# Another order of the first two tiles' work in the opening attention of a two-layer network

## The reference, cut to what matters

```
features_n = rmsnorm(features, fn_w)                 # rows of ctx
Q = rmsnorm(layernorm(x) @ Wq.T + Wq_b, qn_w)
K = rmsnorm(features_n @ Wk.T + Wk_b, kn_w)
attn = softmax(Q @ K.T / sqrt(512))                  # 64 x 64 in each of 32 sequences
x = x + attn @ features_n
...                                                  # sparse ffn, second attention, gated ffn
```

## Time and profile before

| | |
|---|---|
| median of 3 runs | 1487.09 us (1485.61 to 1487.6) |
| span of the profiled execution | 1487.2 us; no other time of that execution is given |
| PE busy | 1456.9 us, 98% of the span |
| DVE, ACT, POOL busy | 1121.6, 793.4 and 708.2 us |
| mean granted clock of TensorE | 0.999 |
| first 45 us: busy PE, DVE, ACT, POOL | 36.9, 27.1, 27.0, 28.7 us |

### The profile page before, as it was taken

The page is one execution under the profiler, slowest core; times in us unless marked ns, Lnnn a source line. Parts: engine busy times, 40 slices in busy tenths (PEclk is TensorE's granted clock), DMA queues, the critical chain, the costliest instruction groups (busy, mean ns, idle before and its releaser), DMA issues.

```text
span 1487.2 us, 27765 instructions
## 1 busy us (share of the span) xinstructions
PE 1456.9 (98%) x9948; PEld 851.1 (57%) x9948; DVE 1121.6 (75%) x2161; ACT 793.4 (53%) x3201; POOL 708.2 (48%) x668
## 2 busy tenths in 40 slices
PE   8999999999999989999999999999999999999998
PEld 6888645555555555556555555655555565555554
DVE  5887787888877878676776776777677677677868
ACT  5678731211123776565556646655754664565663
POOL 6678885554665453344233434333343433343553
PEclk9999999999999999999999999999999999999999
DMA  5744445443444585534443543543454345234523
GB/s 191 239 150 141 128 90 116 106 94 82 75 82 72 118 167 90 125 86 76 110 79 66 108 99 54 102 89 78 89 93 89 82 84 106 51 66 70 103 48 114
DMA packets 359225, 148.98 MB, mean 100 GB/s; under 512 B 342336, under 2 KB 342720, under 8 KB 356144
## 3 DMA queue, kind: packets, MB, share of 16 engines
q1 hardware_dynamic: 357792, 139.87, 44.2%
q10 hardware_dynamic: 1296, 7.34, 1.5%
HBM read 60.11 MB, written 4.19 MB: 43 GB/s over the span
## 4 chain that ended last, share of the span: by engine, by line
PE 49%; DVE 6%; ACT 5%; POOL 3%; DMA 2%; SPq 1%; issue 1%; DVEq 0%; POOLq 0%; ACTq 0%
PE bank L72 16%; PE bank L73 15%; PE bank L74 15%; ACT a_prob L1977 3%; PE bank L2649 2%; DMA a_kT_lo<-a_kn_lo 2%; ACT a_oT_lo L1954 1%; POOL a_qrs L1849 1%; DVE a_oT_lo L2246 1%; ACT a_qr_hi L1951 1%; POOL a_prob L1831 1%; DVE a_kn L2201 1%; DVE a_qve L2185 1%; DVE x_res L2169 1%; DVE x_res L2333 1%
## 5 line engine op out<-in xcount | busy, mean ns | idle before, releaser
L1977 ACT ACTIVATE a_prob<-a_prob,a_nmx 128x64 f32<-128x64 f32 x512 | 170.2, 334 | 250.0 <-DVE a_nmx L2222 249.9
L1831 POOL TENSOR_TENSOR a_prob<-a_prob,a_mask 128x512 f32<-128x512 f32 x64 | 79.9, 1269 | 278.4 <-DVE a_prob L2216 278.4
L72 PE MATMUL bank<-w,xT_hi 128*128 128x448 f16 (+1 forms) x512 | 187.5, 366 | 1.1 <-PEq L1043 1.1
L74 PE MATMUL bank<-w,xT_hi 128*128 128x448 f16 (+1 forms) x512 | 187.3, 366 | 0.0
L73 PE MATMUL bank<-w,xT_lo 128*128 128x448 f16 (+1 forms) x512 | 187.2, 366 | 0.0
L1849 POOL TENSOR_TENSOR a_qrs<-a_qve,neg_half 128x8 f32<-128x8 f32 x64 | 104.2, 1645 | 138.9 <-DVE a_qve L2185 138.6
L1251 ACT CAST f_h_hi<-h 128x448 f16<-128x448 f32 x64 | 35.6, 563 | 207.2 <-DVE h L1325 207.1
L2169 DVE SCALAR_TENSOR_TENSOR x_res<-bank,a_oinv,x_res 128x512 f32<-128x512 f32 x128 | 95.4, 746 | 64.2 <-PE bank L74 64.2
L2174 DVE SCALAR_TENSOR_TENSOR a_qr_lo<-bank,a_qr_hi 128x512 f16<-128x512 f32 x128 | 87.9, 687 | 46.4 <-ACT a_oT_lo L1954 27.4
L1837 POOL TENSOR_TENSOR a_p_hi<-a_prob,a_rden 128x512 f16<-128x512 f32 x64 | 69.5, 1086 | 104.3 <-DVE a_rden L2230 104.3
L1189 POOL TENSOR_TENSOR f_h_lo<-h,f_h_hi 128x448 f16<-128x448 f32 x64 | 72.8, 1141 | 88.9 <-ACT f_h_hi L1251 88.9
(11 more groups left out here) (355 smaller groups left out, 4439.3 us busy)
## 6 DMA issues: line engine op xcount, KB each, us to landing
shared<-in_l_wq SPq DMA_DIRECT2D x8, 1024.0 KB, 4.9
shared<-in_l_wo SPq DMA_DIRECT2D x8, 1024.0 KB, 5.2
shared<-in_w ACTq DMA_DIRECT2D x8, 896.0 KB, 4.7
craw<-in_w SPq DMA_DIRECT2D x11, 512.0 KB, 3.8
a_wide<-in_l_ctxT SPq DMA_DIRECT2D x16, 256.0 KB, 4.0
x_res<-in_x SPq DMA_DIRECT2D x16, 256.0 KB, 4.4
shared<-in_ctx SPq DMA_DIRECT2D x16, 256.0 KB, 4.3
shared<-in_l_wkv SPq DMA_DIRECT2D x8, 512.0 KB, 4.0
```

Of the source, the lines that this page charges most:

```text
L72: pe.matmul(out, a_hi, b_hi, start=first, stop=False)
L74: return pe.matmul(out, a_hi, b_lo, start=False, stop=last)
L1831: pool.tensor_tensor(blocks(prob[u][:, :]), blocks(prob[u][:, :]), mask[:, :].unsqueeze(1).broadcast_to([P, NB, S]), ALU.add).then_inc(s_m ...
L1977: ins = act.activation(pt, pt, ACT.Exp, bias=nmx[:, col:col + 1], accum_out=den[:, col:col + 1])
```

## The change

All five prologues are put in another order. No instruction is added or dropped, and the main loop stays as it is.

- SP: x of tile 0 is loaded between the two halves of `l0_wk`, and ctx of tile 0 ahead of `l0_wq` instead of behind it.
- POOL: `key_root(0)` stands ahead of `features_T(1)`.
- ACT: `squares_c(0)` and `normalise(0)` stand ahead of the first block of `l0_wq`, whose other three blocks now follow `rows_T(0)`; `key_squares(0)` precedes `features_T(1)`; `q_T(0)` and `k_T(0)` precede `squares_c(1)` and `normalise(1)`.
- DVE: after one block of `l0_wq` come `rows_T(0)` and `key_bias(0)`, then three blocks, `wqk`, `query_bias(0)`, `scale_keys(0)`; `statistics(1)` follows these, and `statistics(2)` follows `rows_T(1)`.
- PE: of the four parts of `project_k(1)` one stands ahead of `q_T(0)` and three stand behind `k_T(0)` (before: two ahead, one between, one behind).

```diff
         load_cT(0)
-        for e, ks in enumerate(halves):
-            sp.dma_start(w_raw[1][:, ks, :], a.l0_wk[:, ks, :]).then_inc(wk_in[e], 16)
+        sp.dma_start(w_raw[1][:, halves[0], :], a.l0_wk[:, halves[0], :]).then_inc(wk_in[0], 16)
         load_x(0)
+        sp.dma_start(w_raw[1][:, halves[1], :], a.l0_wk[:, halves[1], :]).then_inc(wk_in[1], 16)
+        load_c(0)
         for e, ks in enumerate(halves):
             sp.dma_start(w_raw[0][:, ks, :], a.l0_wq[:, ks, :]).then_inc(wq_in[e], 16)
-        load_c(0)
...
         first_features_root(0)
+        key_root(0)
         features_T(1)
-        key_root(0)
         first_row_root(1)
...
-        split_wq((0, 1))
+        squares_c(0)
         normalise(0)
-        squares_c(0)
+        split_wq((0,))
         rows_T(0)
-        split_wq((2, 3))
+        split_wq((1, 2, 3))
+        key_squares(0)
         features_T(1)
-        key_squares(0)
+        q_T(0)
+        k_T(0)
         squares_c(1)
-        q_T(0)
         normalise(1)
-        k_T(0)
         rows_T(1)
...
-        split_wq((0, 1))
+        split_wq((0,))
+        rows_T(0)
+        dve.wait_ge(bk_in, 16)
+        key_bias(0)
+        split_wq((1, 2, 3))
         dve.wait_ge(const_in, 32)
         dve.scalar_tensor_tensor(wqk, qnw[:, :], float(D) ** -0.5, wqk, ALU.mult, ALU.mult).then_inc(wqk_ok, 1)
-        rows_T(0)
-        split_wq((2, 3))
-        dve.wait_ge(bk_in, 16)
-        key_bias(0)
-        statistics(1)
+        dve.wait_ge(wqk_ok, 1)
+        dve.wait_ge(off_ok, 2)
         dve.wait_ge(bq_fnw_in, 32)
         query_bias(0)
-        dve.wait_ge(wqk_ok, 1)
-        dve.wait_ge(off_ok, 2)
         scale_keys(0)
+        statistics(1)
         q_T(0)
-        statistics(2)
         k_T(0).then_inc(s_kTl, 1)
         rows_T(1)
+        statistics(2)
         run(body)(dve)
...
-        project_k(1, ks=range(0, 2))
+        project_k(1, ks=range(0, 1))
         q_T(0)
-        project_k(1, ks=range(2, 3))
         k_T(0)
-        project_k(1, ks=range(3, KD))
+        project_k(1, ks=range(1, KD))
         rows_T(1)
```

More of the change, by code:

```diff
@@ L649, in split_wq @@
         def split_wq(ks):
-            act.wait_ge(wq_in[ks[0] // 2], 16)
             for k in ks:
+                act.wait_ge(wq_in[k // 2], 16)
                 act.copy(w_hi[0][:, k, :], w_raw[0][:, k, :]).then_inc(wh_ok, 1)
-        split_wq((0, 1))
+        squares_c(0)
         normalise(0)
-        squares_c(0)
+        split_wq((0,))
         rows_T(0)
-        split_wq((2, 3))
+        split_wq((1, 2, 3))
+        key_squares(0)
         features_T(1)
-        key_squares(0)
+        q_T(0)
+        k_T(0)
         squares_c(1)
-        q_T(0)
         normalise(1)
-        k_T(0)
         rows_T(1)
```

## The result

The changed kernel takes 1489.46 us (median of 17 runs, 1488.09 to 1491.29); the kernel before took 1487.44 us in the 17 runs beside them (1485.11 to 1488.68). The ratio is 1.0015, with a 95% interval of 1.0009 to 1.0021: by the ratio the change costs 2.2 us, between 1.3 and 3.1 (the medians differ by 2.0). That is inside the forecast range of 1486.0 to 1490.0, 1.0 us above the forecast of 1488.5 and 0.2 us above the forecast's own range. It lies between the forecast and rival B.

A forecast was written before the change was run, and what follows sets the result against it. POOL's root for tile 2 was taken to set the rest: other edits gain 0.0, the late statistics cost 1.0 to 1.6 us, taken as 1.4, giving 1488.5 us (chance 0.62). Range 1486.0 to 1490.0.

The forecast's parts named there:

- rival B: Clock falls behind PE's idle gaps near 29 us, adding 1.7 us to the 1.4 delay: 1490.2 us, chance 0.07.
- the forecast's own range: The narrower range around the forecast of 1488.5 us, without the rivals: 1487.9 to 1489.3 us.
- What bounds: POOL's root for the rows of tile 2, at 24.84 us, sets the rest of the run.
- The loads: First loads: the later second half of the key weights costs nothing; turned rows of tile 0 gain 0.31 us.
- First query projection: On PE, begins about 1.1 us earlier, at 15.2, but gains only 0.0 to 0.3 us at its end.
- Keys of tile 0 and features of tile 1: On POOL, key root slowed to 1.4 to 1.6 us, features of tile 1 later; PE gets a new wait of 1.0 us.
- strict case: Port lock taken strictly: scaling the keys of tile 0 waits for POOL until 19.6; the sum is 0.3 us higher.
- Turning, and the rows of tile 1: PE turns the rows of tile 1 at 23.5, as before; queries of tile 1 start perhaps 0.5 us earlier.
- Statistics of tile 2: On DVE, now behind the rows of tile 1, ending at 26.34; POOL's root is delayed 1.0 to 1.6 us.
- Every step of the chain above follows with the same waits: From POOL's root of tile 2 onward, the delay passes unchanged to PE's L913, expected at about 43.6 us.
- A: POOL's chain has slack or tile 1's rows come much earlier; PE's shorter waits count: 1486.5 us, chance 0.18.
- C: The transfer of ctx of tile 3 takes up POOL's delay; the time stays 1487.1 us, chance 0.13.

The follow-up runs named there:

- e1: Changed kernel with statistics(2) put back ahead of k_T(0) on VectorE: 1487.31 us, ratio 0.9998 to the kernel before.
- e2: Kernel before with one edit alone, statistics(2) moved behind rows_T(1) on VectorE: 1488.85 us, ratio 1.0008.
- e5: Changed kernel with statistics(1) ahead of query_bias(0) on VectorE, squares_c(1) and normalise(1) ahead of q_T(0) on ScalarE, statistics(2) left late: 1489.91 us, ratio 1.0012.
- e6: As e5, but with statistics(2) ahead of k_T(0) on VectorE: 1486.67 us, ratio 0.9998 to the kernel before.
- e7: e6 with statistics(2) and POOL's root of tile 2 earlier, normalise(2) ahead of features(0), rows_T(1) between parts of the key projection: 1486.66 us, ratio 0.9994.
- e8: Changed kernel with the loads in the order of the kernel before: 1490.37 us, ratio 1.0017 to the kernel before.
- e9: Kernel before with one edit alone, the new order of the loads: 1487.34 us, ratio 0.9997.
- e10: e7 with weigh(0) and weigh(1) earlier on POOL, bq and fnw loaded ahead of qnw and knw, features(0) behind features_T(1): 1487.59 us, ratio 1.0000.
- e3: Changed kernel with 14 and 9 filling transposes in PE's waits, ahead of the keys of tile 1 and probabilities of tile 0: 1490.43 us, ratio 1.0024.
- e4: Kernel before with the same 14 and 9 filling transposes at the same two places as e3: 1490.03 us, ratio 1.0016.

## Why the prediction was right, and where its size was off

**What bounds.** POOL's root of tile 2 was named as the place from which the rest is set. e1, e2 and the pair e5 and e6 each move the statistics alone, which this root waits for, and the time goes with them, by 2.5, 1.2 and 2.1 us, by their ratios (1.2 by itself is not clear of none). So it is shown that a later root costs. The other direction is not shown: with the root 0.8 us (e6) or 2.3 us (e7) earlier no gain over the kernel before could be measured.

**The loads.** Forecast at no cost; e8 and e9 confirm it. The second half of the key weights was forecast at 9.03; ACT began on it at 9.46, and DVE's third weight block at 10.22 against 9.86. PE's matmuls on it, and the filling transposes behind them, began 0.4 us later than before (12.52 against 12.14), so the rows of tile 0 were turned at 13.39 and not at 13.17: the gain of 0.31 us was 0.09. Nothing of it reached the end.

**First query projection.** Start forecast 15.2, measured 15.39; DVE's blocks forecast to end at 17.7, measured 15.92 + 1.89 = 17.81; the projection's last matmul, at 18.61, ends about half a microsecond later than forecast. From 16.65 its last nine matmuls run back to back, so PE itself was the limit there, and not DVE's last block.

**Keys of tile 0 and features of tile 1.** The key root was forecast at 1.4 to 1.6 us and took 16.89 to 18.21, 1.3 us; L416 ended at 18.18 + 1.36 = 19.54 (forecast 19.6). PE's wait was 0.67 us instead of 1.0, because the projection ended later. The small power took 0.87 us (0.55 before) and the instruction ahead of it 0.37 (0.19), beside DVE's weight splitting. VectorE's three subtractions beside them took 1.89 us, their normal 0.63 each, so the lengthening of 0.3 and 0.2 us fell on POOL alone. By the lock that the Trainium skill describes in "SBUF — State Buffer", section "SBUF: two separate sides", the later one waits until the other instruction is done; the trace is in line with it, since 0.3 us is less than one subtraction. The strict case's extra 0.3 us can't be told from this profile: VectorE came to the scaling of the keys at 19.75, when POOL's pass had ended at 19.54.

**Turning, and the rows of tile 1.** Forecast at 23.5 on PE, measured 23.54. The queries of tile 1 began 0.51 us ahead of their old time; forecast 0.5.

**Statistics of tile 2.** Forecast end 26.34, measured 26.18 + 0.18 = 26.36; the root forecast at 26.4, measured at 26.45. The delay was 1.61 us. The term had been taken at 1.4, nearer to the upper end of 1.0 to 1.6; the upper end was right. The time alone could not tell this: 1.4 lies inside the interval of 1.3 to 3.1 us.

**The waits of PE.** Forecast 1.7 and 1.1 us near 29 to 33; measured 1.71 and 1.15. The list of waits of TensorE up to 150 us, against the earlier trace rows:

```profile
PE bank L913 <- DVE a_wide L696: 5.0, 6, 1.7
...
PE bank L969 <- ACT a_prob L579: 1.1, 1, 1.1
PE bank L72 <- POOL a_big L416: 0.7, 1, 0.7
PE bank L72 <- DVE a_big L683: 0.3, 1, 0.3
PE bank L72 <- DVE a_big L851: 0.3, 1, 0.3
```

The 1.1 us for the first turned rows is gone, and 0.3 + 0.3 + 0.7 stand in its place: one in front of the query projection, one inside it, and the last behind it.

**What was off** is the end of "Every step of the chain above follows with the same waits". Up to POOL's roots of tile 1 the steps did follow, by 1.6 to 1.7 us; but PE's L913 of tile 2 was forecast at 43.6 and came at 44.59, 2.35 us late and without its wait, because the clock had fallen. The condition was named, "it decides if these gaps together do what the one of 2.1 us did", but given only 0.07, as rival B. In the profiled execution the clock does fall, and by e8 the wait of 1.7 us can do it by itself. The price was put at 1.7 us, half of a stretch of 3.4 us; the stretch was 6.8 us long and its slow matmuls cost 2.4 us, but only 0.74 us of that was left at L913, since a wait that PE had anyway took up the most. The Trainium skill's "TensorE: Matmul & The Clock Gate", section "HAM oscillation — how this bites in real kernels", puts such a fall down to idle gaps in front of the work; the trace agrees in that waits of 1.71 and 1.15 us stand there.

Over many runs the clock shows as well. The kernels with the late statistics had mean granted clocks of 0.9972 (the changed kernel), 0.9978, 0.9975 and 0.9972 (e2, e5, e8); the 91 runs of the kernel before had 0.9985, and e1, e6, e7 and e9 0.9985 to 0.9993 (e10, with a long wait of its own, 0.9980). Within one kernel, runs with a lower mean clock are slower: of those 91 runs, the 51 at 0.997 or 0.998 took 1488.2 us on average and the 40 at 0.999 or 1.000 took 1487.0. Fitted inside each kernel over 221 runs, 0.001 of mean clock goes with 0.60 us (standard error 0.08). The changed kernel's 0.0013 below the kernel before is then worth 0.8 us, an estimate worked out from these. With the 2.2 us measured, 1.4 us are left for the delay itself, against 1.61 us read at the root and a forecast of 1.4; with an interval of 1.3 to 3.1 us on the loss, so close an agreement is luck. That is a correlation and an account, not an experiment: the kernels that were to be the experiment, e3 and e4, had a price of their own. Shown is that the place of the statistics makes the whole loss; how it divides between the late root and the clock is only estimated.

**The other rivals.** A asked for L913 of tile 2 at or below 42.24, and C too; it came at 44.59, and both fell. The transfer of ctx of tile 3 was waited for just as long, by the timeline of ScalarE (2.52 us against 2.55 in the earlier trace rows), only 1.72 us later. It is let go by `weigh(1)` and `squares_c(1)`, as the prediction has it; in general by `weigh(n-2)` and `squares_c(n-2)`, and not by `weigh(n-1)`, as the description of the kernel says.

```profile
38.56 0.63 ACT L499 ACTIVATE shared<-shared 128x512 f32<-128x512 f32 x1 [2.52 <-DMA shared<-in_ctx]
```

## What to carry to other kernels

In an order written by hand, look for the engine whose queue hands work to and fro with another without a pause, and ask of every input of that queue whether it is still ready before its turn; here two instructions of 0.9 us, put two steps further back on an engine that was a quarter idle, cost 2.2 us, and the other edits together cost nothing that could be measured. Getting early work done earlier gains nothing while the step that sets the pace stays (e5), and moving that step earlier won nothing that could be measured either, since the next step took over (e6, e7). And a longer wait of the busiest engine can cost more than its length, since the clock may fall behind it; price it by what waits are left behind it to take it up.

## What the runs showed of the hardware that was not expected

- With waits of 1.71 and 1.15 us, which end 2.4 us apart, the clock went to 1.2 GHz for 6.8 us, from early in the second wait; in e1 waits of 0.46 and 1.14 us at the same place did not do this. Where the first wait was 1.7 us the low stretch differed between kernels: 32.3 to 39.1 us in the changed kernel, 32.7 to 36.1 in e5, 31.1 to 37.9 in e8. In e2 the waits were 1.36 and 1.15 us, and the matmuls behind them took 0.39 us; there the clock was at 0.50 only from 44 to 47 us, behind the third wait, of 1.44 us at 42.67. Behind the same third wait it stayed at 1.00 in the profiles of the kernel before, e1, e3, e6, e7 and e9 (1.44 to 1.46 us). So waits of 1.4 to 1.8 us are followed by the lower level in some executions and not in others.
- The stretch at 1.2 GHz behind 538 us comes in some executions and not in others: the clock from 538 to 541.4 us was 0.50 in the profile of the kernel before and 1.00 in that of the changed kernel, e1 and e2; of all twelve profiles six were below 1. From L913 of tile 2 to the end of the span it is 1443.0 us in the changed kernel without it and 1445.0 us in the kernel before with it. A single profiled span says little about a change of 2 us for that reason.
- The first loads land over 1 us apart between executions of the same order: with the old order of loads, DVE's third key weight block began at 9.86 in the kernel before, at 8.62 in e8 and at 11.34 in e4. The 17 runs of the kernel before lie 3.6 us apart.
- Twenty-three small matmuls put near 30 us cost the kernel before 2.4 us (ratio 1.0016, 1.0008 to 1.0025), for a reason not found.
